# Weaving the mask rows, the context counts and the turn of the first x1 blocks into the last attention block, and running the first scores two blocks ahead

## What is computed

```
n1 = layernorm(x)                                   # no gain
z  = softmax(causal and padded (n1 Wq1)(n1 Wk1)^T / sqrt(32)) (n1 Wv1)
x1 = layernorm(n1 + z) * ln1_g + ln1_b
# cross attention: keys of the context, length = how many energies of query row 0 are not 0
z  = softmax(padded (x1 Wq2)(ctx Wk2)^T / sqrt(32)) (ctx Wv2)
x2 = layernorm(x1 + z) * ln2_g + ln2_b
y  = layernorm(x2 + relu(x2 fc1_w + fc1_b) fc2_w + fc2_b) * ln3_g + ln3_b
x3 = x + tanh(g_xattn) * y
out = x3 + tanh(g_ffn) * (n + 0.5 * (silu(h w1 + b1) w2 + b2)),   n = layernorm(x3),
                                                    h = layernorm(n) * gamma + beta,
                                                    w1, w2: int codes times scales
```

## Time and profile before

| | |
|---|---|
| time, median of 3 runs | 1770.26 us (1767.98 to 1770.68) |
| the profiled execution | 1767.68 us, of which the span of the trace is 1765.9 us |
| mean granted TensorE clock | 0.981 of full |
| PE busy | 1685.2 us, 95% of the span |
| DVE, ACT, POOL busy | 833.6, 549.6, 358.6 us |
| the chain that ended last | PE 85%, DVE 7%, ACT 2%, POOL 2%, DMA 2% |

### The profile page before, as it was taken

One profiled execution on the slowest core, in us unless ns is written; L12 is line 12 of the kernel. 1 busy time (PEld: TensorE's weight loads), 2 busy tenths in 40 slices (PEclk: granted clock), 3 DMA queues, 4 the chain that ended last, 5 costly groups with the idle time before them and its releaser, 6 DMA issues.

```text
span 1765.9 us, 20630 instructions
## 1 busy us (share of the span) xinstructions
PE 1685.2 (95%) x7806; PEld 1375.2 (78%) x7806; DVE 833.6 (47%) x1696; ACT 549.6 (31%) x964; POOL 358.6 (20%) x509
## 2 busy tenths in 40 slices
PE   6998999999889999889999899999999999999999
PEld 5776888887778888667787677878788787878787
DVE  4555544467365544468888865332322323232311
ACT  4221112122112211265665443332222323222322
POOL 0111110013011100058888920100000000000000
PEclk9899999999999999889999989999999999999999
DMA  6211111123011111544554342201010101000000
GB/s 186 72 41 64 62 54 37 36 72 90 19 68 58 55 36 36 161 154 156 161 163 165 114 144 89 66 1 48 1 48 1 48 1 34 14 24 24 1 24 24
DMA packets 68822, 117.22 MB, mean 66 GB/s; under 512 B 11201, under 2 KB 13249, under 8 KB 68571
## 3 DMA queue, kind: packets, MB, share of 16 engines
q1 hardware_dynamic: 64968, 110.12, 19.2%
q10 hardware_dynamic: 3757, 5.80, 1.0%
HBM read 81.05 MB, written 34.84 MB: 66 GB/s over the span
## 4 chain that ended last, share of the span: by engine, by line
PE 85%; DVE 7%; ACT 2%; POOL 2%; DMA 2%; issue 1%; ACTq 0%; SPq 0%; DVEq 0%; POOLq 0%
PE banks L637 79%; PE banks L647 3%; PE banks L764 2%; DVE split_q L1479 1%; DVE split L1479 1%; DVE plain L1974 1%; ACT split_q L994 1%; DVE split L1939 1%; DVE plain L2017 1%; DMA plain<-in_L_xattn_Wq 1%; ACT split L994 1%; DMA plain<-in_x 1%; DMA plain<-in_L_xattn_fc_w 0%; DVE plain L1637 0%; POOL split L1372 0%
## 5 line engine op out<-in xcount | busy, mean ns | idle before, releaser
L637 PE MATMUL banks<-split_q,split 128*128 128x512 f32 x2304 | 573.5, 399 | 4.7 <-POOL split L1372 4.5
L637 PE MATMUL banks<-split 128*128 128x512 f32 (+4 forms) x2292 | 549.6, 390 | 28.4 <-DVE split L1479 15.5
L637 PEld LDWEIGHTS banks<-split 128*128 128x128 f32 (+3 forms) x2292 | 415.8, 187 | 130.9 <-issue 21.8
L637 PEld LDWEIGHTS banks<-split_q,split 128*128 128x128 f32 x2304 | 433.0, 191 | 94.8 <-POOL split L1372 6.1
L637 PE MATMUL banks<-split,split_q 128*128 128x512 f32 (+3 forms) x1824 | 421.1, 386 | 5.4 <-DVE split_q L1479 2.8
L637 PEld LDWEIGHTS banks<-split,split_q 128*128 128x128 f32 x1824 | 329.7, 193 | 66.0 <-DVE split_q L1479 3.7
L1479 DVE TENSOR_TENSOR split<-banks,split 128x512 fp32r<-128x512 f32 (+5 forms) x232 | 147.4, 641 | 189.6 <-ACT split L994 189.2
L994 ACT ACTIVATE split<-banks 128x512 fp32r<-128x512 f32 (+5 forms) x232 | 124.6, 557 | 324.0 <-PE banks L764 215.3
L1939 DVE TENSOR_TENSOR split<-plain,split 128x512 fp32r<-128x512 f32 x128 | 88.5, 691 | 258.7 <-ACT split L1285 258.7
L1279 ACT ACTIVATE plain<-banks,small 128x512 f32<-128x512 f32 x128 | 87.6, 684 | 284.7 <-PE banks L637 284.7
L1479 DVE TENSOR_TENSOR split_q<-banks,split_q 128x512 fp32r<-128x512 f32 x68 | 46.7, 687 | 253.0 <-ACT split_q L994 253.0
(11 more groups left out here) (150 smaller groups left out, 1226.2 us busy)
## 6 DMA issues: line engine op xcount, KB each, us to landing
plain<-in_x SPq DMA_DIRECT2D x64, 256.0 KB, 2.8
xo_scratch<-plain SPq DMA_DIRECT2D x32, 256.0 KB, 2.0
x_scratch<-plain SPq DMA_DIRECT2D x32, 256.0 KB, 2.0
plain<-x_scratch SPq DMA_DIRECT2D x32, 256.0 KB, 2.9
tile_x<-xo_scratch SPq DMA_DIRECT2D x32, 256.0 KB, 3.1
xg_scratch<-tile_x SPq DMA_DIRECT2D x32, 256.0 KB, 2.0
out<-plain SPq DMA_DIRECT2D x32, 256.0 KB, 2.1
tile_x<-x_scratch SPq DMA_DIRECT2D x28, 256.0 KB, 4.5
```

The source lines that it names most:

```text
L637: mm = nc.tensor.matmul(out, left(c, l), right(c, r), start=start and c == 0 and (l, r) == PASSES[0], stop=stop and c == chunks - 1 and (l ...
```

## The change

1. In the first group (blocks 0 to 3) the scores run two blocks ahead: S(2) stands before V(0), S(3) before V(1), and Q(1,0) before V(2).
2. From block 4 on, in rows that do not open a group, B of the block before is moved from behind the first S of the row to behind its last S (before the last V).
3. In batch 1's last row (i = 15) new entries do work of the next stage: R (PE counts the rows; on POOL the low half of `rows_1`), C (DVE counts), Y (turn of x1 block c of tile 0), K (lengths on PE, masks on DVE). Only batch 1 has them. The x1 blocks are now turned from `N[:, 0]`, which is free earlier than `x1b`.
4. The loads for this leave ACT's queue and what followed the SP loop, and go into SP's loop at i = 13, 14 and 15; fc1_w alone stays with ACT.
5. B(15) of batch 1 is done on DVE after tile 0's `add_z`; the split of fc1 is placed around the softmax of tile 0; the x1 blocks of tile 1 are turned around `turn_probs(0)`.

The core of the diff (`...` marks what is left out):

```diff
 def attention_order():
-    order = [("S", 0, 0), ("X", 0, 0)]
-    for i in range(NB):
+    order = [("S", 0, 0), ("X", 0, 0), ("S", 1, 0), ("X", 1, 0), ("T", 0, 0), ("S", 2, 0), ("X", 2, 0), ("V", 0, 0),
+             ("T", 1, 0), ("S", 3, 0), ("X", 3, 0), ("A", 0, 0), ("V", 1, 0), ("B", 0, 0), ("T", 2, 0), ("Q", 1, 0),
+             ("A", 1, 0), ("V", 2, 0), ("Q", 1, 1), ("B", 1, 0), ("Q", 1, 2), ("A", 2, 0), ("Q", 1, 3), ("B", 2, 0),
+             ("T", 3, 0), ("S", 4, 0), ("S", 4, 1), ("X", 4, 0), ("V", 3, 0)]
+    for i in range(4, NB):
...
         elif n1:
-            order += [("T", i, 0), end[0], ("S", i + 1, 0), end[1]]
+            order += [("T", i, 0), end[0], ("S", i + 1, 0)]
...
-            order.append(("V", i, n0 - 1))
+            order += [end[1], ("V", i, n0 - 1)]
         else:
-            order += [("L", i, 0), ("L", i, 1), ("T", i, 0), ("M", i, 0), ("T", i, 1), ("M", i, 1), ("V", i, 0),
-                      end[0], ("N", i, 0), ("T", i, 2), ("V", i, 1)]
+            order += [("L", i, 0), ("L", i, 1), ("R", i, 0), ("T", i, 0), ("M", i, 0), ("T", i, 1), ("M", i, 1),
+                      ("C", i, 0), ("V", i, 0), end[0], ("N", i, 0), ("Y", i, 0), ("T", i, 2), ("V", i, 1)]
             order += [("W", i, c) for c in range(C)]
-            order += [("N", i, 1), ("T", i, 3), end[1], ("V", i, 2), ("V", i, 3), ("L", i, 2), ("M", i, 2)]
+            order += [("N", i, 1), ("Y", i, 1), ("T", i, 3), ("V", i, 2), end[1], ("Y", i, 2), ("Y", i, 3), ("K", i, 0),
+                      ("V", i, 3), ("L", i, 2), ("M", i, 2)]
...
@@ SP, in the loop over the blocks @@
+                    if i == NB - 3 and b + 1 == B:
+                        sp.wait_ge(z_free, 2 + b * NB + 3 * C)
...
+                    if i == NB - 2 and b + 1 == B:
+                        sp.wait_ge(tp_full, TURNS["p", b, NB - 2, 3] + 1)
+                        for k in range(BT):
+                            load_n(0, 0, k)
+                        sp.wait_ge(s_full, B * SS1)
+                        sp.wait_ge(parked, 32)
+                        for b_ in range(B):
+                            sp.dma_start(G[:, b_:b_ + 1].rearrange("p s c h n -> p s (c h n)").bitcast(F32),
+                                         g_dram[b_:b_ + 1].rearrange("b p n -> p b n")).then_inc(g_in[b_], 16)
...
+                    if i == NB - 1 and b + 1 == B:
+                        for k in range(BT):
+                            load_x1b(1, k)
...
                     sp.wait_ge(x1_ready, b * NB + i + 1)
                     sp.dma_start(x1_dram[b * S + i * P:b * S + (i + 1) * P, :], U[:, i % 2]).then_inc(
                         x1_out[i % 2], 16)
...
@@ PE @@
+            def count_rows():
+                pe.wait_ge(s_free, 2 + B * SS1)
+                for b in range(B):
+                    pe.wait_ge(g_in[b], 16)
+                pe.wait_ge(rows_lo, 1)
...
+                    elif kind == "R" and b + 1 == B:
+                        count_rows()
+                    elif kind == "Y" and b + 1 == B:
+                        turn_x1(0, c)
+                    elif kind == "K" and b + 1 == B:
+                        count_lengths()
...
-            turn_x1(0, 0)
-            turn_x1(0, 1)
-            count_lengths()
-            turn_x1(0, 2)
-            turn_x1(0, 3)
-            pe.wait_ge(fcw_in[0], 16)
-            b1_shift(0)
+            pe.wait_ge(mm_free, 2 + MM2)
             pe.wait_ge(c_free, 1)
             cross_scores(0)
+            pe.wait_ge(fcw_in[0], 16)
+            b1_shift(0)
...
@@ DVE @@
+            split_fc1((0, 1))
             softmax(0)
+            split_fc1((2, 3))
             sum_probs(0)
+            lo_x1(1, 0)
+            lo_x1(1, 1)
             lo_probs(0)
+            lo_x1(1, 2)
+            lo_x1(1, 3)
+            for k in range(BT):
+                add_z(0, k)
+            end_b(NB - 1)
```

More of the change, by code:

```diff
@@ L163, in probs_at @@
 def probs_at(t):
-    return TP2 + 9 * t + 4
+    return TP2 + (9 * t + 4 if t else 6)
 def x1_at(t, k):
-    return TP2 + (9 * t - 4 + k if t else k)
+    return TP2 + 9 * t - 4 + k - (1 if t == 1 and k < 2 else 0) if t else TURNS["x1", 0, k, 0]
 def x2_at(t, k):
@@ L536, in load_unit @@
                     load_w2(n - 16)
[L538 to L549, removed]
             sp.wait_ge(fcw_lo, C)
@@ L703, in _, with count_lengths, turn_x1 @@
                 k += 1
+            def count_rows():
[3 more added lines that the diff above has]
+                pe.wait_ge(rows_lo, 1)
+                for b in range(B):
+                    mm = product(PS[0:1, 0, b * SCP:(b + 1) * SCP], lambda c, h: rows_1[:, h, b, c:c + 1],
+                                 lambda c, h: G[:, b, c, h, :], C)
+                mm.then_inc(c_full, 1)
+            def count_lengths():
+                pe.wait_ge(counted, B + 1)
+                nc.tensor.matmul(PS[:, 1, 0:B], ones, keys_seen2[0:1], start=True, stop=True).then_inc(c_full, 1)
+            def turn_x1(t, k):
+                n = x1_at(t, k)
+                if t:
+                    pe.wait_ge(x1b_in[k], t * 16)
+                else:
+                    pe.wait_ge(n_in[0][k], 16)
+                pe.wait_ge(tp_free, n + 1)
+                x = x1b if t else N[:, 0]
+                turn(PS[:, 2 + n % 2], lambda c: x[:, k, c * P:(c + 1) * P])
             for b in range(B):
@@ L777, in _ @@
                         turn_x(b + 1, c)
[L780 to L787, removed]
-            mm.then_inc(c_full, 1)
-            def count_lengths():
-                pe.wait_ge(counted, B + 1)
-                nc.tensor.matmul(PS[:, 1, 0:B], ones, keys_seen2[0:1], start=True, stop=True).then_inc(c_full, 1)
-            def turn_x1(t, k):
-                n = x1_at(t, k)
-                pe.wait_ge(x1b_in[k], t * 16 + 16)
-                pe.wait_ge(tp_free, n + 1)
-                turn(PS[:, 2 + n % 2], lambda c: x1b[:, k, c * P:(c + 1) * P])
+                    elif kind == "R" and b + 1 == B:
+                        count_rows()
+                    elif kind == "Y" and b + 1 == B:
+                        turn_x1(0, c)
+                    elif kind == "K" and b + 1 == B:
+                        count_lengths()
             def cross_scores(t):
@@ L1544, in lo_x, with lo_t, lo_x1, count_rows @@
                 lo(n, halves[1], quarters(PS[:, 2 + n % 2]), halves[0])
+            def lo_t(k, dst, k_bank, turn=0, per=0):
+                lo(k, dst[1], quarters(PS[:, 2 + k_bank % 2]), dst[0], turn, per)
+            def lo_x1(t, k):
+                n = x1_at(t, k)
+                lo_t(n, [x1T[:, :, h, k * P:(k + 1) * P] for h in range(2)], n)
+            def count_rows():
+                dve.wait_ge(c_full, 1)
+                for b in range(B):
+                    ins = nc.vector.tensor_scalar(S2[0:1, b, 0:SC], PS[0:1, 0, b * SCP:b * SCP + SC], 0.0, None,
+                                                  ALU.not_equal, ALU.add, accum_out=keys_seen2[0:1, b:b + 1])
+                    if b == 0:
+                        p0.done(ins)
+                ins.then_inc(c_free, 1)
+                dve.wait_ge(c_free, 1)
+                p0.wait()
+                nc.vector.tensor_copy(sum2[0:1, 0:1], keys_seen2[0:1, 0:1]).then_inc(counted, 1)
+            def mask_contexts():
+                dve.wait_ge(c_full, 2)
+                p0.link(nc.vector.tensor_copy(len2, PS[:, 1, 0:B]))
+                for b in range(B):
+                    p0.done(nc.vector.tensor_scalar(mask2[:, b], keys[:, 0:SC], len2[:, b:b + 1], -BIG,
+                                                    ALU.is_ge, ALU.mult))
+                p0.wait()
+                p0.link(nc.vector.reciprocal(rc2[:, 0:B], len2))
+                p0.link(nc.vector.tensor_scalar(rc2[:, 0:B], rc2[:, 0:B], 0.0, None, ALU.mult))
+                p0.link(nc.vector.tensor_tensor(mask2[:], mask2[:],
+                                                rc2[:, 0:B].unsqueeze(2).to_broadcast([P, B, SC]), ALU.add))
+                nc.vector.tensor_copy(sum2[:, 0:1], len2[:, 0:1]).then_inc(len_seen, 1)
             def lo_wv(b, c):
@@ L1698, in _, with split_fc1 @@
             R2 = 2 * NB * B
[L1700 to L1708 removed]
+            def split_fc1(chunks):
+                for c in chunks:
                     dve.wait_ge(fcw_hi, c + 1)
```

186 lines of the change are left out of this document (77 added, 109 removed).

## The result

The changed kernel took 1773.99 us (median of 8 runs, 1768.47 to 1776.96), the kernel before 1769.33 us in the runs beside it. The ratio is 1.0029, 95% interval 1.0019 to 1.0039: slower by 4.7 us, where 1768 and no measurable change had been forecast. The profiled execution took 1773.74 us, its span is 1772.0 us against 1765.9.

A forecast was written before the change was run, and what follows sets the result against it. PE's work, waits and clock were taken as the bound (PE 85% of the chain). Terms -6.8 - 2.2 + 8.7 - 1.9 = -2.2 us, from 1770.3, gave 1768, no measurable change (chance 0.40); 8-in-10 range 1762 to 1776.

The forecast's parts named there:

- First group: Blocks 0 to 3, scores two ahead: fewer PE waits, -2.7 us per batch, -1.4 for one low-clock spell; together -6.8.
- The rest of the group has no wait that I can find: First group after V(2): low half of T(3) at 176.8, before V(3) at 177.35; T(4,0) at 180.1, -2.7 us.
- the walk: Step-by-step timing of the new order; in batch 0's first group from T(0) at 148.6, with V(2) at 162.35.
- B behind the last S: Rows 4 to 14: T(5,0) loses its 1.12 us wait in each batch, -2.2 us, bounds 0 and -2.2.
- What is queued behind B(13): Row 15 of batch 0: SP's later loads delay V(15,0) by 7.1 us, plus 1.6 of low clock; together +8.7.
- Row 15 of batch 1 and after the last V: PE stands 10.1 us for G before R; after the last V, `mlp_in` comes at 767.5 against 769.42, -1.9 us.
- until the first `add_z` it gets a little longer: Stretch after the last V: 9.6 us to first `add_z` (before 8.5), then 12.1 to `mlp_in` (before 14.7).
- (a): Rival, chance 0.24: kinder clock, no low spells after the two long waits or in batch 1's first group; 1763.5 us.
- (b): Rival, chance 0.10: the chain over B(13) holds nobody, since the loads arrive in time; 1748 us.
- (c): Rival, chance 0.26: clock stays low after PE's 10 us wait in batch 1's row 15; 1775 us, or 1776.6.

The follow-up runs named there:

- b13_low_first: Changed kernel with B(13) back behind S(15,0), and B(0), B(2) behind the low halves of T(2,0), T(3,0): 1743.09 us, ratio 0.9857.
- first_group_only: Kernel before with only the first group's new order (scores two ahead, Q(1,0) before V(2)): 1764.41 us, ratio 0.9972.
- b_late_only: Kernel before with only B(i - 1) moved behind the last S in rows 4 to 14: 1776.10 us, ratio 1.0034.
- g_first: Changed kernel with SP issuing G's two DMAs ahead of the four x1 loads at i = 14: 1770.22 us, ratio 1.0004.
- b13_probs_first: Changed kernel with B(13) back behind S(15,0) and the turn of the probabilities ahead of tile 1's x1 turns: 1754.5 us, ratio 0.9911.
- r_later: Changed kernel with R moved behind V(15,0) and C behind N: 1768.10 us, ratio 0.9989.
- low_b1_late: `b13_low_first` with `b1_shift(2)` and `(3)` moved behind the cross values: 1748.9 us, ratio 0.9886.
- low_cross_late: `b13_low_first` with `cross_scores(1)` behind the first two x2 turns instead of ahead of them: 1744.72 us, ratio 0.9866.
- b13_early: Changed kernel with B(13) alone back at its old place behind S(15,0): 1753.85 us, ratio 0.9903.

## Why the prediction was wrong

The direction was missed because two of four terms were too kind; the costly one was right. Against the timed runs the first group was 2.1 us too kind, row 15 with the stretch behind it 4.3, and the late B 0.5.

- **First group, -6.8 forecast, -4.7 measured alone** (0.9961 to 0.9983), and -2.5 in the pair of traces. The failed step is "The rest of the group has no wait that I can find", and with it the full clock at which the walk took V(2). In batch 0 the 2.7 us of the walk went into V(2), 1.45 longer at the low clock, and into 1.54 of wait before V(3). The low half of T(3,0), set at 176.8, came at 179.45: it stands behind B(2), B(2) behind POOL's root, the root behind `make_xo(3)`, that behind the load of x that SP issues after B(1). `b13_low_first` shows it by taking B(2) out of that line. In the trace of `first_group_only` batch 0 has gained 0.2 us at its T(4,0), batch 1 another 4.0 at its own.
- **B behind the last S, -2.2.** The waits of 1.12 us before T(5,0) went in both batches, as forecast.
- **What is queued behind B(13), +8.7.** Right: +6.7 and +1.7 in the trace. With the -2.2, +6.5 forecast and +7.0 measured by `b_late_only`.
- **Row 15 of batch 1 and after the last V, -1.9 forecast, +3.5 in the trace, +2.4 by difference of the timed runs.** The mechanism stood as written (B(13), SP's chain, four loads, G, R). Four sizes were off. G landed 6.8 after its issue and not 4.7: +2.1; `g_first` shows that 2.5 of the 6.8 come from the 1 MB in front. R and the turns ran at half clock: +1.1. The V after them did not: -1.5. And the stretch from the cross scores on took 28.5 and not 24.8: +3.7. (The walk's own terms add up to 727.06 for V(15,0), not 726.95.)
- **The failed step in that stretch** is "until the first `add_z` it gets a little longer (...: 9.6), from there to `mlp_in` shorter (...: 12.1)". Measured were 12.8 (750.16 to 762.93) and 13.0. I had given it the better half of either order: in `b13_probs_first` the two are 10.0 and 18.0. Some 1.2 us of the 3.7 is clock: `g_first` and `r_later` have the same code there, make the second 8 matmuls of `b1_shift` in 1.89 us instead of 3.16, and take 27.4 and 27.3. For the rest no single engine is shown to be the cause. PE's own order counts, since 3.3 us more in front of the x2 turns made the stretch 3.4 longer (`low_b1_late`). But taking `cross_scores(1)` from in front of the first ones did not make it shorter, for then the norm of the last block ended last (`low_cross_late`). The cause of the remaining 2.5 us stays open.
- **The rivals.** (a) came in small part: R's spell was over before V(15,0), the others were there (4.87 for V(15,0) of batch 0; 0.61 and 0.54 granted from 482 to 490, and V(2) in 3.21 instead of 2.33, in batch 1). (b) is refused by `b13_early`. (c) gave 1775 and slower, near the measured time, by a mechanism that did not occur: after 12 us of wait the clock was back for the first full product. So it is luck that the measured 1774 lies in the range of 1762 to 1776, whose upper part was there for (c). The profile's windows over PE (stretch, length, busy, granted clock, DMA share, GB/s):

```profile
716.00:728.00 12.00, 0.78 (x4) 0.74 0.72 235
728.00:732.00 4.00, 3.08 (x31) 0.50 0.25 76
732.00:736.00 4.00, 3.17 (x15) 1.00 0.01 4
```

## What to carry to other kernels

A step that is moved past the last product of a row moves everything that another queue issues after it: follow the semaphore that the step sets through every in-order queue until something that has no order of its own, and do it for the rows at the ends of the loop first, where the queue carries the next stage's loads. A weave that fills a wait must have its operands behind nothing new; here the fill was worth having only once its input stood ahead of the chain. And when a reorder takes one wait away, walk on to the end of the group over all engines: the instruction next in line had a root, the making of xo and a load in front of it.

## What the runs showed of the hardware

The granted clock fell where PE was busy. In the changed kernel's windows behind the cross scores PE works nearly all the time, at first on matmuls with one output column and turns, and from 761 on at half clock on full products as well:

```profile
748.00:752.00 4.00, 4.00 (x28) 1.00 0.74 237
752.00:756.00 4.00, 4.00 (x24) 0.56 0.85 278
756.00:768.00 12.00, 10.63 (x34) 0.50 0.01 5
```

And after a long wait it came back while only small matmuls ran (0.50 in 728 to 732, 1.00 from 732 on). A wait of 2.9 us before V(2) was followed by a low spell in the changed kernel (3.74 us) and by none in `b13_early` (2.32 us), so single spells of 1.5 us are not something to forecast. The run times of one kernel go with the clock, if only roughly: `b13_early` took 1745.14 and 1746.88 at a mean of 0.989 and 0.988, and 1753.05 to 1757.96 at 0.981 to 0.984; its profile is of its fastest run, which is why waits and not spans are compared here.
